# A decoder layer on one core: the experts' tiles change from 256 to 128 rows, each expert's first tile leaves the loop, and second choices are gathered by batch

## The chip, the core and the metric

The program runs on one core of a Trainium2 chip. The core has five engines that run side by side: TensorE (PE for its matmuls, PEld for its loads of stationary operands), VectorE (DVE), ScalarE (ACT), GpSimd (POOL) and SyncE (SP), and 16 DMA engines that move data. The metric is the device time of one execution in microseconds (us). Lower is better.

## What is computed

The reference is one decoder layer on x of shape (8, 224, 512) in float32: a Mamba block, cross-attention on a context of 750 rows, and a mixture of four experts. Each of the three adds its result to x. The change touches the last one:

```python
def _L0_ffn_ref(x, rW1, rb1, rW2, rb2, We1, be1, We2, be2):   # x: (8, 224, 512), We1: (4, 512, 2048), We2: (4, 2048, 512)
    rh = jax.nn.gelu(x @ rW1 + rb1, approximate=False)
    router_probs = jax.nn.softmax(rh @ rW2 + rb2, axis=-1)
    expert_weights, expert_indices = jax.lax.top_k(router_probs, 2)
    one_hot = jax.nn.one_hot(expert_indices, E, dtype=x.dtype)
    token_mask = one_hot.sum(axis=2)
    combine_w = (one_hot * expert_weights[..., None]).sum(axis=2)
    out = jnp.zeros_like(x)
    for e in range(E):
        xi = x * token_mask[..., e:e + 1]
        h = jax.nn.gelu(xi @ We1[e] + be1[e], approximate=False)
        yo = h @ We2[e] + be2[e]
        out = out + yo * combine_w[..., e:e + 1]
    return out
```

Every one of the 1792 rows takes two of the four experts, so 3584 rows go through an expert. Evaluated on its inputs, the reference sends 383, 1011, 1368 and 822 rows to experts 0 to 3.

## The kernel before

The program has four stages, one function each: `mamba_in`, `state_space`, `attention` and `experts`. The attention stage ends with the router. It gives each row two slots in `xs_d`, a table in device memory with 1792 slots for each expert, scatters the normed rows there (L1316), and counts each expert's tiles into `tiles_i` (`count_tiles`, L1464 on: `taken` compares the tile starts with the number of rows, `tiles[:, 0]` has the tiles of an expert and `tiles[:, 1]` the tiles before it).

`experts` (L1884) then does for each expert the tiles that its count asks for. Every engine runs the same frame, `expert_tiles` (L1969): read the two counts into registers (`counts`, L1965, its loads are L1967), do `first`, then a loop over all EG possible tiles of the expert (L1975) in which a branch (L1976) skips the tiles that aren't taken. EG is 7, since a tile has GT = 256 rows.

A tile is worked as follows.
- SP loads the tile's rows of `xs_d` into `xt` (L1994), one tile ahead. PE turns them by transposes with the identity (`tokens`, L2210, eight for a tile). The program keeps float32 accuracy by splitting every operand into a high part of type fp32r and the low rest. ACT writes the high part `xTh` (L2164) and DVE the low part `xTl` (L2116).
- The hidden layer has 2048 columns in HC = 16 chunks of 128. For chunk c, PE does the first layer: four blocks of the contraction with three products each (`products`, L2198 to L2200: high by high, high by low, low by high), so 12 matmuls. The stationary operand is a 128x128 block of the weights `w1h` or `w1l`, and the rows of the tile move, 256 of them. ACT applies the Gelu twice (L2173 for the high part `hh`, L2174 back into `ps`), and DVE takes the difference `hl` (L2124).
- PE does the second layer of chunk c two chunks later (AHEAD = 2): here `hh` and `hl` are stationary and the 512 columns of `w2h` or `w2l` move. A tile has two halves of 128 rows (HALVES = 2), so 6 matmuls.
- After the last chunk DVE adds the bias (L2131) into `y`, and ACT's queue stores it back into `xs_d` (L2177).

A product's three matmuls and what stands in which operand:

```python
(sh, sl), (mh, ml) = stationary, moving
nc.tensor.matmul(out, sh, mh, start=first, stop=False)
nc.tensor.matmul(out, sh, ml, start=False, stop=False)
return nc.tensor.matmul(out, sl, mh, start=False, stop=last)
```

Weights come in chunks of 1 MB into `stage` (eight for each expert). The first chunks of expert 0 are split into high and low by ACT (L2155) and DVE (L2099), all later ones by POOL (L2024 high, L2026 low), which waits for the last use of the buffer by the expert before. The first split of the tokens of an expert and the two counts stand between the last tile of one expert and the first of the next. DVE also works out the gates (L2103 to L2105) before its first `hl`.

At the end the two results of each row are added to the attention's output: POOL gathers the first choices by index while the last expert works (`gather`, L2052 into `early`; scaled in L2068, added in L2070), and when the last tile is stored it gathers the second choices of all 16 groups of 112 rows (L2052 into `back`, which is a view of `w1l`). DVE adds them (L2146), and SP (L2005) and ACT (L2189) store the output.

## Time and profile before

| what | value |
|---|---|
| three runs | 2640.47, 2632.47, 2620.92 us (median 2632.47 us) |
| the profiled execution | 2644.08 us |
| its span, first to last instruction | 2642.3 us |
| mean granted TensorE clock | 0.949 of 2.4 GHz |
| PE busy | 2374.5 us (90% of the span), 14400 matmuls |
| PEld busy | 2006.9 us (76%) |
| DVE, ACT, POOL busy | 1458.0 us (55%), 1237.7 us (47%), 1383.3 us (52%) |
| `experts` | from about 1793 us of the span to its end |

PE is busy through most of the span; how much of that is real work for the array the busy share doesn't say, since matmuls are pipelined and their shown lengths overlap. The pace of matmuls is therefore read from starts: how many start in how many us. A row's idle time is that of its engine just before the instruction, with what released it. The 1.7 us between the span and the execution's time are launch and end.

### The profile page before, as it was taken

The numbers are of one execution on the slowest core, as the hardware profiler recorded it, in microseconds if no ns is written. First come the engines' busy times: TensorE is split into PE (matmuls) and PEld (weight loads), VectorE is DVE, ScalarE is ACT, GpSimd is POOL, SyncE is SP. The second block draws the span as 40 slices with busy tenths as digits, with TensorE's granted clock in tenths as the row PEclk, the third lists the DMA queues.
The fourth block names the chain that finished last, engine by engine and source line by source line (L and its number), as shares of the span: only waits on it lengthen the run. The fifth ranks groups of instructions, "written<-read, shape, count | busy, mean of one in ns | idle before, by whom it ended". The sixth has DMA issues, their size and how long they took to land. (4 is left out here: it accounts for less than half of the span.)

```text
span 2642.3 us, 39584 instructions
## 1 busy us (share of the span) xinstructions
PE 2374.5 (90%) x14400; PEld 2006.9 (76%) x14400; DVE 1458.0 (55%) x2036; ACT 1237.7 (47%) x2659; POOL 1383.3 (52%) x952
## 2 busy tenths in 40 slices
PE   6999589999999998799999998975999989998994
PEld 5867389999999995566676666645888888888883
DVE  7804589999999993556776667634211211211212
ACT  4335477778877752344454445323233233333331
POOL 2413477877787871555656565635640640019812
PEclk9999789999999999799999999877999999999997
DMA  4326856656676564644555455415220220003303
GB/s 109 135 65 212 261 177 206 195 178 207 202 209 198 171 202 129 174 113 111 129 137 137 111 128 132 124 35 174 92 91 16 87 96 16 24 31 104 109 27 119
DMA packets 235987, 341.74 MB, mean 129 GB/s; under 512 B 34702, under 2 KB 164302, under 8 KB 234686
## 3 DMA queue, kind: packets, MB, share of 16 engines
q1 hardware_dynamic: 213246, 279.89, 37.2%
q0 software_dynamic: 13728, 47.19, 5.6%
q10 hardware_dynamic: 8864, 12.72, 1.4%
q8 instruction: 87, 1.43, 0.2%
q14 instruction: 62, 0.51, 0.1%
HBM read 212.08 MB, written 127.65 MB: 129 GB/s over the span
## 5 line engine op out<-in xcount | busy, mean ns | idle before, releaser
L956 DVE TENSOR_TENSOR_SCAN s_h<-s_decay,s_ub 128x928 f32<-128x928 f32 x256 | 527.5, 2080 | 17.5 <-PE s_ub L983 7.8
L994 PE MATMUL s_yps<-s_hc,identity 128*128 128x224 f32 x2016 | 425.8, 354 | 3.2 <-POOL s_hc L829 2.8
L2124 DVE TENSOR_TENSOR e_hl<-e_ps,e_hh 128x256 fp32r<-128x256 f32 x256 | 108.6, 425 | 571.5 <-ACT e_ps L2174 571.0
L882 ACT ACTIVATE s_decay<-s_dt,s_A 128x224 f32<-128x224 f32 x1024 | 387.9, 472 | 1.6 <-DMA s_dt<-dt_d 1.6
L994 PEld LDWEIGHTS s_yps<-s_hc,identity 128*128 128x128 f32 x2016 | 363.8, 191 | 5.4 <-POOL s_hc L829 4.7
L1338 DVE TENSOR_REDUCE t_nmax<-t_ps 112x1 fp32r<-112x752 f32 x256 | 240.2, 938 | 219.4 <-PE t_ps L1677 218.7
L1294 POOL TENSOR_TENSOR t_part<-t_pT 125x672 f32<-125x672 f32 x128 | 207.1, 1618 | 271.3 <-ACT t_pT L1582 268.9
L2173 ACT ACTIVATE e_hh<-e_ps,e_b 128x256 fp32r<-128x256 f32 x256 | 122.0, 477 | 433.0 <-PE e_ps L2200 432.8
L2198 PE MATMUL e_ps<-e_xTh,e_w1h 128*128 128x256 f32 x1024 | 293.1, 286 | 24.1 <-DVE e_xTl L2116 24.1
L1582 ACT ACTIVATE t_pT<-t_ps 125x448 f32<-125x448 f32 x384 | 181.1, 546 | 254.8 <-PE t_ps L1703 251.3
L2199 PE MATMUL e_ps<-e_xTl,e_w1h 128*128 128x256 f32 x1024 | 292.0, 285 | 0.0
L2200 PE MATMUL e_ps<-e_xTh,e_w1l 128*128 128x256 f32 x1024 | 291.0, 284 | 0.0
L829 POOL TENSOR_TENSOR s_hc<-s_h,carry 128x896 f32<-128x896 f32 x128 | 248.0, 1950 | 71.1 <-DVE s_h L956 49.7
L829 POOL TENSOR_TENSOR s_hc<-s_h,s_Cc 128x896 f32<-128x896 f32 x128 | 248.0, 1948 | 68.4 <-DVE s_h L956 49.7
L2024 POOL TENSOR_TENSOR e_w1h<-carry,e_one 128x2048 fp32r<-128x2048 f32 x13 | 46.9, 3611 | 376.5 <-PE e_ps L2200 376.3
L2198 PE MATMUL e_ps<-e_w2h,e_hh 128*128 128x512 f32 x512 | 206.0, 402 | 22.4 <-DVE e_hl L2124 22.4
L2198 PEld LDWEIGHTS e_ps<-e_xTh,e_w1h 128*128 128x128 f32 x1024 | 197.6, 193 | 35.0 <-issue 25.2
L1677 PE MATMUL t_ps<-t_k,t_q 96*112 96x376 f32 x512 | 186.9, 448 | 31.4 <-DVE t_nmax L1338 23.3
L2199 PEld LDWEIGHTS e_ps<-e_xTl,e_w1h 128*128 128x128 f32 x1024 | 197.4, 193 | 9.3
L2200 PE MATMUL e_ps<-e_w2h,e_hl 128*128 128x512 f32 x512 | 202.7, 396 | 0.0
L2199 PE MATMUL e_ps<-e_w2l,e_hh 128*128 128x512 f32 x512 | 202.2, 395 | 0.0
L2200 PEld LDWEIGHTS e_ps<-e_xTh,e_w1l 128*128 128x128 f32 x1024 | 198.9, 194 | 0.0
(242 smaller groups left out, 4611.2 us busy)
## 6 DMA issues: line engine op xcount, KB each, us to landing
s_ut<-ut_d SPq DMA_DIRECT2D x192, 128.0 KB, 3.3
carry<-in_L_ffn_We POOLq DMA_DIRECT2D x24, 1024.0 KB, 5.7
t_k<-kh_d SPq DMA_DIRECT2D x64, 375.0 KB, 6.5
xs_d<-s_zero SPq DMA_DIRECT2D x30, 512.0 KB
ut_d<-a_x SPq DMA_DIRECT2D x32, 448.0 KB, 5.5
kh_d<-s_kh SPq DMA_DIRECT2D x32, 375.0 KB, 3.0
kl_d<-s_kl SPq DMA_DIRECT2D x32, 375.0 KB, 3.6
v_d<-s_v SPq DMA_DIRECT2D x48, 250.0 KB
```

The costliest lines, as they stand in the source:

```text
L829: nc.gpsimd.tensor_tensor(hc[:, u % 2, k], h[:, k, :, 2:SLOT], Cc[b % 2][:, k], ALU.mult).then_inc(hc_done, 1)
L882: ins = nc.scalar.activation(decay[:, u % 2, :, n, 2:SLOT], dts[:, u % 2].rearrange("p (s t) -> p s t", s=NSEG), ACT.Exp, scale=A[:, u % C ...
L956: nc.vector.tensor_tensor_scan(h[:, k].rearrange("p n t -> p (n t)"), decay[:, u % 2, k].rearrange("p n t -> p (n t)"), ub[:, s % 2, AT:AT ...
L994: ins = nc.tensor.matmul(yps[:, u % 2, 0:L], ident[:], hc[:, u % 2, :, n], start=(n == 0), stop=(n == NS - 1))
L1294: nc.gpsimd.tensor_tensor(part[:], p[:, 0:3], p[:, 3:6], ALU.add).then_inc(sum_step, 1)
L1338: nc.vector.tensor_reduce(nmax[:, u, h:h + 1], ps[0:TT, 0:2, 0:EVEN], AX.XY, ALU.max, negate=True).then_inc(max_done, 1)
L1582: nc.scalar.activation(pT[:, g % PT, 2 * i:2 * i + 2], ps[0:CT, TURN_BANK + i, 0:2 * L].rearrange("p (i t) -> p i t", i=2), ACT.Exp).then_ ...
L1677: ins = nc.tensor.matmul(ps[0:TT, i, 0:EVEN], q3[0:ROWS3, b % 2, h, u * TT:(u + 1) * TT], k3[0:ROWS3, J % 2, h % 4, i * (CTX - EVEN):i * ( ...
L2173: nc.scalar.activation(hh[:, c % RING], hidden_in, ACT.Gelu, bias=bias).then_inc(S["h_high"], 1)
L2198: nc.tensor.matmul(out, sh, mh, start=first, stop=False)
L2199: nc.tensor.matmul(out, sh, ml, start=False, stop=False)
L2200: return nc.tensor.matmul(out, sl, mh, start=False, stop=last)
```

## The change

Tiles have 128 rows (GT = 128, EG = 14), so `xt`, `xTh`, `xTl`, `hh`, `hl` and `y` are half as long, a first-layer matmul moves 128 columns instead of 256, and a second-layer chunk has 3 matmuls instead of 6. The second layer runs three chunks behind (AHEAD = 3). The rows of a tile are turned at its step 8 instead of at its end.

Each expert's first tile is written out ahead of the loop (`first`), with rows of its own (`xf`, `fTh`, `fTl`, bank 7 of `ps`), which PE turns at step 12 of the first tile of the expert before and which ACT and DVE split at that tile's end. The loop has EG - 1 = 13 iterations, and `taken` counts only the tiles after the first.

The weights' chunks are split anew between the engines: POOL splits the first-layer chunks and an expert's first second-layer chunk; ACT and DVE split the other three second-layer chunks in halves, among the hidden chunks 1, 5 and 9 of an expert's first tile (for expert 0 chunks at 5, 9 and 13). `w2h` and `w2l` have a fifth part so that the next expert's first chunk has a place. SP loads these chunks, `b2` comes one expert at a time, and SP rather than ACT stores `y`.

Second choices are gathered by batch: DVE works out how many tiles of the last expert cover the rows of each of the batches 0 to 6 (`last_tiles`), and POOL waits for that many stores, gathers, scales and adds the two groups of that batch and stores its output, while the last expert still works. Only the last batch's two groups come after the last tile.

On PE the order within a tile changes. These are the rows in the loop's body around a second-layer chunk, in the kernel before (`e_w1h`, `e_w1l`, `e_w2h`, `e_w2l` are the weights, `e_ps` the banks that are written):

```order
L2200 MATMUL e_ps<-e_xTh,e_w1l 128x256
L1932 REGISTER_ALU
L2198 MATMUL e_ps<-e_w2h,e_hh 128x512
L2199 MATMUL e_ps<-e_w2l,e_hh 128x512
L2200 MATMUL e_ps<-e_w2h,e_hl 128x512
L2198 MATMUL e_ps<-e_w2h,e_hh 128x512
L2199 MATMUL e_ps<-e_w2l,e_hh 128x512
L2200 MATMUL e_ps<-e_w2h,e_hl 128x512
L2198 MATMUL e_ps<-e_xTh,e_w1h 128x256
```

And in the changed kernel, at the same place of its loop's body:

```order
L2298 MATMUL e_ps<-e_xTh,e_w1l 128x128
L1939 REGISTER_ALU
L2296 MATMUL e_ps<-e_w2h,e_hh 128x512
L2297 MATMUL e_ps<-e_w2l,e_hh 128x512
L2298 MATMUL e_ps<-e_w2h,e_hl 128x512
L2296 MATMUL e_ps<-e_xTh,e_w1h 128x128
```

The second layer has half as many rows for a tile of half the size. The first layer has 12 rows for each chunk in both (one ahead and one behind are shown here), each with half the moving columns.

The second place is POOL's end of the program. Before, it ends with the counts of the last expert and sixteen gathers (`e_w1l` is where `back` lies):

```order
L2068 TENSOR_SCALAR e_early<-e_early,e_gate 112x512
L2070 TENSOR_TENSOR carry<-carry,e_early 112x512
L1967 TENSOR_LOAD r_tiles_i
L1967 ISA x2
L1967 TENSOR_LOAD r_tiles_i
L1967 ISA x2
L1932 ISA
L2052 DMA e_w1l<-xs_d,r_index 112x512 x16
```

Now it ends with the last of seven batches and two gathers:

```order
L2104 DMA e_early<-xs_d,r_index 112x512 x2
L2113 TENSOR_SCALAR e_early<-e_early,e_gate 112x512
L2115 TENSOR_TENSOR carry<-carry,e_early 112x512
L2113 TENSOR_SCALAR e_early<-e_early,e_gate 112x512
L2115 TENSOR_TENSOR carry<-carry,e_early 112x512
L2134 DMA out<-carry 112x2x512
L1986 TENSOR_LOAD r_tiles_i
L1986 ISA x2
L1986 TENSOR_LOAD r_tiles_i
L1986 ISA x2
L1939 ISA
L2104 DMA e_early<-xs_d,r_index 112x512 x2
```

Fourteen of the sixteen gathers moved ahead of the wait for the last tile, with their scaling and adding, and these are POOL's now instead of DVE's.

The core of the diff:

```diff
-GT = 2 * P
+GT = P
...
-                nc.vector.tensor_reduce(tiles[:, 0, 0:E], taken[:], AX.X, ALU.add).then_inc(counted, 1)
+                nc.vector.tensor_reduce(tiles[:, 0, 0:E], taken[:, :, 1:EG], AX.X, ALU.add).then_inc(counted, 1)
...
-    AHEAD = 2
-    HALVES = GT // P
+    AHEAD = 3
+    EARLY = 3
...
-        w2h, w2l = (sb(n, [P, WG, CW, DM], F32R) for n in ("w2h", "w2l"))
+        w2h, w2l = (sb(n, [P, WG + 1, CW, DM], F32R) for n in ("w2h", "w2l"))
...
+        FROM_START = ((0, 0, 0), (0, 0, 1), (0, 1, 0), (0, 1, 1))
+        AMONG = [{5: (0, 2, 1), 9: (0, 3, 0), 13: (0, 3, 1)}] + [{1: (e, 1, 1), 5: (e, 2, 1), 9: (e, 3, 1)} for e in range(1, E)]
+        BY_ACT = list(FROM_START) + [AMONG[e][c] for e in range(E) for c in sorted(AMONG[e])]
+        BY_POOL = [(0, 2, 0), (1, 0, 1)] + [(e, g, 0) if g < WG else (e + 1, 0, 1) for e in range(1, E) for g in range(WG + (e + 1 < E))]
...
-            with eng.Fori(0, EG) as i:
+            with eng.Fori(0, EG - 1) as i:
                 with eng.If(i < taken_e):
-                    body(i, before + i, before + e + i)
+                    body(i, before + (e + 1) + i)
...
+                        load(e * EG + 1, n)
+                        wait_split(sp, (e, 0, 1))
+                        load_weights(sp, (e, 2, 1), S["w2_loaded0"])
+                        if e + 1 < E:
+                            load_first(e + 1)
+                            wait(sp, "y_done", n)
+                            load_b2(e + 1)
+                        wait_split(sp, (e, 1, 1))
+                        load_weights(sp, (e, 3, 1), S["w2_loaded1"])
+                    if e + 1 < E:
+                        for g in (2, 3):
+                            wait_split(sp, (e, g, 1))
+                            load_weights(sp, (e + 1, g - 2, 1), S[f"w2_loaded{g % 2}"])
+                    store(e * EG, n)
+                def tile(i, n):
+                    load(i + (e * EG + 2), n)
+                    store(i + (e * EG + 1), n)
+                expert_tiles(sp, e, first, tile)
...
+            split((0, 2, 0))
+            load_next((0, 2, 0))
+            load_next((0, 3, 0))
+            split((1, 0, 1))
             for e in range(1, E):
-                before = counts(pool, e)[1]
-                for n in range(2 * WG * e, 2 * WG * (e + 1)):
-                    g = n % (2 * WG) // 2
-                    wait(pool, "l2_mm" if n % 2 else "h_mm", before * HC + (g + 1) * CW - HC)
+                before = counts(pool, e)[1] + e
+                for g in range(WG):
+                    wait(pool, "h_mm", before * HC + (g + 1) * CW - HC)
                     pool.sem_inc(S["waited"])
-                    split(n)
-            pool.wait_ge(S["w_split"], 2 * WG * E)
+                    split((e, g, 0))
+                    load_next((e, g, 0))
+                if e + 1 < E:
+                    wait(pool, "l2_mm", before * HC)
+                    pool.sem_inc(S["waited"])
+                    split((e + 1, 0, 1))
...
+            for b in range(B - 1):
+                through = pool.value_load(through_i[0:1, b:b + 1], min_val=0, max_val=EG)
+                wait(pool, "y_stored", (before + through) * 16)
+                pool.sem_inc(S["waited"])
+                for i in (2 * b, 2 * b + 1):
+                    gather(1, i)
+                for i in (2 * b, 2 * b + 1):
+                    combine(1, i)
+                pool.wait_ge(S["early_combined"], NT + 2 * b + 2)
+                pool.dma_start(out[b].rearrange("(u p) d -> p u d", p=TT), stage[0:TT, b // 2, 2 * (b % 2):2 * (b % 2) + 2]).then_inc(out_early, 16)
+            total = counts(pool, E)[1] + E
+            wait(pool, "y_stored", total * 16)
             pool.sem_inc(S["waited"])
-            for i in range(NT):
-                gather(1, i, back[:, i // 4, i % 4], r_gathered[i // 4])
+            for i in (NT - 2, NT - 1):
+                gather(1, i)
+            pool.wait_ge(out_early, 16 * (B - 1))
...
+            def low_weights(chunk):
+                high, low = parts(chunk)
+                wait_weights(dve, chunk)
+                for half in range(2):
+                    two = slice(2 * half, 2 * half + 2)
+                    dve.wait_ge(S["w_high"], 2 * BY_ACT.index(chunk) + half + 1)
+                    v.tensor_tensor(low[:, two], raw(chunk)[:, two], high[:, two].bitcast(F32), ALU.subtract).then_inc(S["w_split"], 1)
...
+            def last_tiles():
+                then(v.tensor_scalar(seen[:], slot[0:1, 2:NT:2, E - 1], float(-(E - 1) * SLOTS), None, ALU.add))
+                then(v.tensor_tensor(cover, starts[:].unsqueeze(1).to_broadcast([1, B - 1, EG]),
+                                     seen[:].unsqueeze(2).to_broadcast([1, B - 1, EG]), ALU.is_lt))
+                then(v.tensor_reduce(seen[:], cover, AX.X, ALU.add))
+                v.tensor_copy(through_i[:], seen[:]).then_inc(S["known"], 1)
...
+                        low_hidden(n, c)
+                        if c in AMONG[e]:
+                            low_weights(AMONG[e][c])
+                        if c == 8:
+                            tokens(n)
+                        if e == 1 and c == 12:
+                            last_tiles()
+                    if e + 1 < E:
+                        first_tokens(e + 1)
+                    results(e, n)
+                def tile(i, n):
+                    for c in range(HC):
+                        low_hidden(n, c)
+                    tokens(n)
+                    results(e, n)
...
+            def first_tokens(e):
+                act.wait_ge(S["f_mm"], e + 1)
+                nc.scalar.activation(fTh[:].rearrange("p k t -> p (k t)"), ps[:, F_BANK], ACT.Copy).then_inc(S["f_high"], 1)
...
+                        hidden(e, n, c)
+                        if c in AMONG[e]:
+                            high_weights(AMONG[e][c])
+                        if c == 8:
+                            tokens(n)
+                    if e + 1 < E:
+                        first_tokens(e + 1)
+                def tile(i, n):
+                    for c in range(HC):
+                        hidden(e, n, c)
+                    tokens(n)
...
+            def layer1(e, n, c, xh, xl):
+                g, w = c // CW, slice(c % CW * P, c % CW * P + P)
+                wait(pe, "h_split", n * HC + c - RING + 1)
+                for q in range(KC):
+                    ins = products(ps[:, H_BANK + c % RING, 0:GT], (w1h[:, g, q, w], w1l[:, g, q, w]),
+                                   (xh[:, q], xl[:, q]), q == 0, q == KC - 1)
+                ins.then_inc(S["h_mm"], 1)
+            def layer2(e, n, c):
+                k = c % RING
+                high, low = parts((e, c // CW, 1))
+                if c == 0:
+                    wait(pe, "y_done", n)
+                wait(pe, "h_split", n * HC + c + 1)
+                ins = products(ps[:, Y_BANK], (hh[:, k], hl[:, k]), (high[:, c % CW], low[:, c % CW]), c == 0, c == HC - 1)
+                ins.then_inc(S["l2_mm"], 1)
...
+                def first(n):
+                    pe.wait_ge(S["f_split"], e + 1)
+                    for step in range(HC + AHEAD):
+                        c = step - AHEAD
+                        if step < HC:
+                            if step % CW == 0:
+                                wait_split(pe, (e, step // CW, 0))
+                            layer1(e, n, step, fTh, fTl)
+                        if step == 8:
+                            tokens(n)
+                        if step == 12 and e + 1 < E:
+                            first_tokens(e + 1)
+                        if c >= 0:
+                            if c % CW == 0:
+                                wait_split(pe, (e, c // CW, 1))
+                            layer2(e, n, c)
...
+                def tile(i, n):
+                    wait(pe, "x_split", n)
+                            layer1(e, n, step, xTh, xTl)
+                        if step == 8:
+                            tokens(n)
...
+                            layer2(e, n, step - AHEAD)
```

## Rows read from the trace of the kernel before

**Rows 1.** Chain of waits, pieces by time: start, us, what; two tile ends and the tail
```profile
2210.88 0.87 PE e_ps L2210 x8
...
2258.08 0.87 PE e_ps L2210 x8
...
2605.47 2.79 DMA xs_d<-e_y
...
2609.08 0.99 POOL e_w1l L2052
...
2628.93 7.30 DMA e_w1l<-xs_d,r_index
```

**Rows 2.** Groups of instructions from 1750 us on (busy, mean ns, idle before)
```profile
L2198 PE MATMUL e_ps<-e_xTh,e_w1h 128*128 128x256 f32 x1024 | 293.1, 286 | 24.1 <-DVE e_xTl L2116 24.1
...
L2198 PE MATMUL e_ps<-e_w2h,e_hh 128*128 128x512 f32 x512 | 206.0, 402 | 22.4 <-DVE e_hl L2124 22.4
...
L2173 ACT ACTIVATE e_hh<-e_ps,e_b 128x256 fp32r<-128x256 f32 x256 | 122.0, 477 | 433.0 <-PE e_ps L2200 432.8
...
L2116 DVE TENSOR_TENSOR e_xTl<-e_ps,e_xTh 128x512 fp32r<-128x512 f32 x40 | 25.8, 686 | 23.5 <-ACT e_xTh L2164 23.5
L2068 POOL TENSOR_SCALAR e_early<-e_early,e_gate 112x512 f32<-112x512 f32 x16 | 25.4, 1586 | 0.6
...
L2164 ACT ACTIVATE e_xTh<-e_ps 128x512 fp32r<-128x512 f32 x40 | 21.7, 596 | 4.5 <-PE e_ps L2210 3.5
```

**Rows 3.** Timeline of PE, one chunk's step: start, length, instruction
```profile
2000.96 0.28 PE L2198 MATMUL e_ps<-e_xTh,e_w1h 128*128 128x256 f32 x1
...
2002.38 0.40 PE L2198 MATMUL e_ps<-e_w2h,e_hh 128*128 128x512 f32 x1
...
2003.78 0.28 PE L2198 MATMUL e_ps<-e_xTh,e_w1h 128*128 128x256 f32 x1
```

**Rows 4.** Timeline of PE, runs of narrow matmuls in other stages
```profile
992.84 7.29 PE L1004 MATMUL s_yps<-s_hc,identity 128*128 128x112 f32 x64
...
1200.26 0.27 PE L1689 MATMUL t_ps<-t_turner,t_nmax 112*2 112x112 f32 x2
...
1202.29 0.81 PE L1703 MATMUL t_ps<-t_q,t_k 98*125 98x224 f32 x6
```

**Rows 5.** Lengths of one, ns min/median/max, by line
```profile
L1689 PE MATMUL t_ps<-t_turner,t_nmax x128: 212/217/378, 1047.1 to 1725.6; 112*2 112x112 f32 x128
L1703 PE MATMUL t_ps<-t_q,t_k x768: 263/272/695, 1049.3 to 1729.2; 98*125 98x224 f32 x192
```

**Rows 6.** Groups of weight loads, shapes apart (mean ns before the second bar)
```profile
L2198 PEld LDWEIGHTS e_ps<-e_xTh,e_w1h 128*128 128x128 f32 x1024 | 197.6, 193 | 35.0 <-issue 25.2
...
L1689 PEld LDWEIGHTS t_ps<-t_turner,t_nmax 112*2 112x2 f32 x128 | 11.1, 87 | 7.3 <-issue 2.0
```

**Rows 7.** Busy time by stretch: PE, PEld, DVE, ACT, POOL, granted clock, DMA
```profile
992.70:999.80 7.10, 7.10 (x65) 7.10 (x64) 0.85 (x2) 0.00 (x0) 1.56 (x1) 1.00 0.17 52
```

**Rows 8.** Timelines of ACT and PE around the change from one tile to the next
```profile
2265.73 1.28 ACT L2173 ACT_TABLE_LOAD   x1 [5.66 <-issue]
...
2268.35 0.50 PE L2198 MATMUL e_ps<-e_w2h,e_hh 128*128 128x512 f32 x1 [0.98 <-DVE e_hl L2124]
```

**Rows 9.** Timeline of PE at the change from expert 0 to 1 and 1 to 2
```profile
1913.54 1.09 PE L2210 MATMUL e_ps<-identity,e_xt 128*128 128x128 f32 x8 [1.80 <-issue]
1921.21 0.58 PE L2198 MATMUL e_ps<-e_xTh,e_w1h 128*128 128x256 f32 x1 [6.59 <-DVE e_xTl L2116]
...
2110.92 1.09 PE L2210 MATMUL e_ps<-identity,e_xt 128*128 128x128 f32 x8 [0.30 <-issue]
```

**Rows 10.** Timelines of DVE and POOL at the start of the experts
```profile
1808.25 4.59 DVE L2103 TENSOR_TENSOR e_eq<-r_slot,r_choice 112x64 f32<-112x64 f32 x1
...
1812.88 0.22 DVE L2104 TENSOR_TENSOR e_eq<-e_eq,r_pm 112x64 f32<-112x64 f32 x1
...
1807.50 5.26 POOL L2026 TENSOR_TENSOR e_w1l<-carry,e_w1h 128x2048 fp32r<-128x2048 f32 x1 [13.50 <-ACT e_w1h L2155]
```

More of the change, by code:

```diff
@@ L2080, in _ @@
             start(dve, "step x_split h_split y_done combined")
+            v = nc.vector
             step = [0]
@@ L2191, in _ @@
+            wait(act, "combined", 2)
+            act.dma_start(out_v[NT - 1], stage[0:TT, (NT - 1) // 4, (NT - 1) % 4]).then_inc(S["out_stored"], 16)
         @block.tensor
```

351 lines of the change are left out of this document (173 added, 178 removed).

## The prediction, made before the changed kernel ran

> **What bounds the kernel now.** I read the views in this order: the chain of waits, the groups of instructions, the timeline of PE, and then everything in the trace that tells the pace of a narrow matmul.
>
> The chain ends with 37 us of tail, and before it runs along PE through the experts [rows 1]. The tail: the last tile is stored (2605.47), sixteen gathers are issued one by one from 2609.08, the last lands 7.30 us after 2628.93, and the sums and the store end the span at 2642.3. In front of it, one tile follows the other in 47.2 us (2210.88 to 2258.08). The groups show why: each first-layer product has 1024 matmuls and each second-layer product 512, so 1024 / 64 = 16 tiles ran, and PE's idle time in front of them is 24.1 + 22.4 us in all [rows 2]. So PE bounds this stage: what the change does to the matmuls counts in full, and what it saves elsewhere is at most those 46 us, the cold clock behind them, and the tail.
>
> One step of the loop (a chunk's first layer, and the second layer of another) takes 2.82 us, from 2000.96 to 2003.78 [rows 3]. Its 12 matmuls of 256 columns take 1.42 us, 118 ns each; its 6 of 512 columns take 1.40 us, 233 ns each. Sixteen steps are 45.1 us, eight transposes 0.87 us [rows 1], and the remaining 1.2 us is the wait for the first `hl` of the tile: ACT loads a table for 1.28 us when it starts on the tile, and PE idles 0.98 us for DVE behind that [rows 8].
>
> **The change, part by part.**
>
> *Number of tiles.* The reference sends 383, 1011, 1368 and 822 rows to the experts. In tiles of 256 that is 2 + 4 + 6 + 4 = 16, as the trace has it. In tiles of 128 it is 3 + 8 + 11 + 7 = 29. The rows worked through fall from 4096 to 3712, by 9%.
>
> *Second layer.* Here the tile's rows are the stationary side, and 512 columns still move. So a chunk has 3 matmuls of 233 ns instead of 6: 0.70 us.
>
> *First layer.* The weights are stationary, and each of the 12 matmuls still needs its own load of 128 columns; only the moving side shrinks to 128. What does such a matmul take? The trace has no fp32r matmul with 128 stationary and 128 moving columns, so I bound it.
> - From below, if only its moving columns counted: L1689 moves 112 columns against 2 stationary ones, and the second of a pair starts 0.27 - 0.217 = 0.053 us after the first [rows 4, 5]. From 53 ns at 112 columns to 233 ns at 512 is 0.45 ns for a column, so 60 ns for 128.
> - From above, the 118 ns of today.
> - Nearest rows, with 128 or nearly 128 stationary columns: L1004, which moves 112 columns, runs 64 matmuls in 7.29 us, 0.275 us of which is the last one's own length: 7.02 / 63 = 111 ns. L1703 (fp32r, 125 stationary, 224 moving) starts six in 0.81 - 0.27 = 0.54 us: 108 ns [rows 4, 5]. The load itself lasts 87 ns with 2 columns and 193 ns with 128 [rows 6], so 106 ns more for 126 columns: a load occupies its path for about 108 ns, whatever moves.
>
> I take 111 ns. Halving the moving columns then saves 7 ns of 118, and the first layer, which was done once for 256 rows, is done twice. A chunk's first layer is 12 x 111 = 1.34 us, a step 2.04 us, sixteen steps 32.6 us, and four transposes 0.44 us: 33.0 us for a tile.
>
> The Trainium skill has a rule by which this would come out otherwise: "TensorE: Matmul & The Clock Gate", section "Back-to-back issue gap", gives about 81 ns for each matmul in a sustained stream of loads and matmuls of 128 columns. By it a tile would take 27.2 us. The rows at 108 and 111 ns don't agree with it, so I keep it as a rival.
>
> *From one tile to the next.* With AHEAD = 3 and the rows turned at step 8, what follows the last first-layer chunk is: two activations (under 1 us at 256 columns), the copy of 0.60 us and the subtraction of 0.69 us [rows 2], about 2.3 us in all, beside four second-layer chunks of 0.70 us on PE. ACT's table load lies beside the four first-layer chunks (5.3 us) that now precede the first second-layer one. So I expect most of the 1.2 us to go; bounds 0 and 1.3 us, taken 0.2 us. A tile then takes 33.2 us. Queued behind the subtraction on DVE are the bias and the loop's branch, which nobody waits for before the next tile's first `hl`.
>
> Sum of the tiles: 29 x 33.2 - 16 x 47.2 = 963 - 755 = **+208 us**.
>
> *From one expert to the next.* Each of the three changes costs the kernel before about 10 us over an ordinary tile: PE waits 6.6 us (at the first) for the first split of the tokens, after up to 1.8 us for its own branches, and comes out at half clock (a first matmul of 0.58 us instead of 0.28) [rows 9]. The token wait goes. What is late next is PE's own sequencer: with 5 skipped iterations it was 1.80 us late, with 3 only 0.30 us, so 0.75 us for each one skipped. Of 13 iterations it will skip 11, 6 and 3: 6.3 + 2.6 + 0.3 = 9 us. I add 6 us for the half clock behind the first two and 1.3 us for the extra transposes: 16 us instead of 31, **-15 us**, between -25 and 0.
>
> *Weights on DVE.* The low halves move into the first tile of an expert, beside POOL's splits. A DVE instruction with two inputs in SBUF doesn't run beside POOL: the one at 1808.25 took 4.59 us and ended with POOL's, which had begun at 1807.50 and lasted 5.26 us; the like-sized one behind it took 0.22 us [rows 10]. POOL's splits of the fourth chunk lie in the first 8 us of an expert's first tile, where DVE's first low half falls due; `hl` of the next chunk is queued behind it, and PE has about 4 us in hand. I take 1.5 us for each of three experts, **+4 us**, between 0 and 25 (three times a full split of 8.3 us).
>
> The Trainium skill says of this in "SBUF — State Buffer", section "Who interferes with whom", that GpSimd and such an operation of VectorE exclude each other for a whole instruction. The row of 4.59 us agrees with it. By that rule POOL can also be the one that waits, which would not reach PE here.
>
> *The start.* The gates' instructions no longer wait for two splits of POOL but for one: **-3 us**, between -6 and 0.
>
> *The tail.* Two gathers instead of sixteen remain: 14 x 1.24 us (the mean from 2609.08 to 2628.93 over 16) = 17 us, and a smaller burst lands sooner by some 3 us: **-21 us**, between -17 and -25. The fourteen others go to POOL beside the last expert. At about 1 us to issue and 1.6 us to scale [rows 2], no more to add, a group costs some 4 us, 30 groups 120 us, while the last expert's seven tiles take 232 us. So they hide.
>
> *Sum.* 208 - 15 + 4 - 3 - 21 = **+173 us**. On the profiled execution: 2644.1 + 173 = 2817 us. That execution lies 11.6 us above the median of the three runs, and I forecast against the median: 2632.5 + 173 = **2805 us**, 6.6% slower.
>
> **The rivals.**
>
> *A, the loads hide, and it is faster.* If the next load ran wholly beside the matmul before it, a first-layer matmul would take the 60 ns of its moving columns. There are 29 x 192 = 5568 of them, so 51 ns x 5568 = 284 us less: 2521 us. It decides from 80 ns down: 173 us / 5568 = 31 ns under 111. For it speaks that PEld always runs beside PE; against it both runs of narrow matmuls [rows 4], one in each format.
>
> *B, the loads hide in part.* If 31 of the 51 ns between the two bounds hid, a matmul would take 80 ns and the whole 5568 x 31 ns = 173 us less: 2632 us, no change. The same rows speak against it; for it, that no row has just this shape. The Trainium skill's 81 ns, named above, is nearly this case.
>
> *C, the handover stays.* If ACT's table load and branch still make PE wait 1.3 us a tile, and the matmuls stay at 118 ns as at 256 columns, it is 28 x 1.1 + 5568 x 0.007 = 31 + 39 = 70 us more: 2875 us. The first chunk of a tile is ready four chunks before its use now, which speaks against the wait; that today's 118 ns may come from memory rather than from columns speaks for the pace.
>
> *D, the clock.* The array now streams columns for a smaller part of the time (60 of 111 ns in the first layer). If the granted clock fell to 1.2 GHz in some tiles, each of them would take about 33 us more; five of them make 2970 us. Against it: in the stretch of L1004, which moves 112 columns in 111 ns, the granted clock was 1.00 [rows 7].
>
> **How the numbers follow.** Forecast 0.78, A 0.05, B 0.03, C 0.10, D 0.04. The range goes by the bounds: 108 ns instead of 111 takes 17 us off, and changes between experts without a late sequencer 9 more, with a tail and start at their best 7 more, so 2770; upwards the handover (31), half of the pace to 118 (20) and the collisions' and experts' upper ends in part give 2865. A measurement of this kernel can tell about 1%, 26 us, from no change. Faster by more than that is A (0.05), within it B (0.03), slower the rest (0.92).
>
> **What would show it.** In the changed kernel's profile: 5568 first-layer matmuls with 128x128 outputs that start 111 ns apart, their loads still about 193 ns long; a step of 2.04 us; tiles 33.2 us apart; 29 of them; idle of PE before L2296 with its largest single gaps where experts change, 6 us at the first; `w_split` waits of PE near nothing; two gathers behind the last store and about 16 us from it to the end. It would be wrong if the matmuls start less than 80 ns apart, or if the router's counts give other than 29 tiles (33 us for each).

## The result, and the profile after

The changed kernel takes 2839.45 us, the median of four runs from 2829.45 to 2844.61, beside 2632.89 us for the kernel before. The medians lie 207 us apart; the ratio on record is 1.0763, with an interval from 1.0732 to 1.0795, which is 201 us of the time before. 173 us had been forecast. The sign and the main mechanism (more matmuls at nearly the same pace each) were as forecast. The sum came out 28 us short by the ratio and 34 by the medians, and behind that stand larger errors of both signs.

The groups of instructions of the changed kernel, from 1780 us on (line, engine, operation, shapes, count, busy us and mean ns, idle before), answer to [rows 2] and [rows 6]:

```profile
L2298 PE MATMUL e_ps<-e_xTh,e_w1l 128*128 128x128 f32 x1600 | 440.2, 275 | 0.0
...
L2296 PEld LDWEIGHTS e_ps<-e_xTh,e_w1h 128*128 128x128 f32 x1600 | 305.8, 191 | 15.2
...
L2296 PE MATMUL e_ps<-e_w2h,e_hh 128*128 128x512 f32 x464 | 209.1, 451 | 4.1 <-DVE e_hl L2193 4.0
...
L2298 PE MATMUL e_ps<-e_fTh,e_w1l 128*128 128x128 f32 x256 | 88.1, 344 | 0.0
```

The first-layer matmuls are split over two tiles (`xTh` in the loop, `fTh` in an expert's first tile) and over three lines for the three products. 3 x (1600 + 256) = 5568 of them ran, so there were 29 tiles, as forecast; 464 / 16 = 29 says the same of the second layer. A load still takes 191 ns. The groups already hold a warning: a matmul of the same shape lasted 275 ns in the loop and 344 ns in the first tiles.

One step in the timeline of PE (start, length, instruction), the counterpart of [rows 3]:

```profile
2024.27 0.22 PE L2296 MATMUL e_ps<-e_xTh,e_w1h 128*128 128x128 f32 x1
2024.32 0.28 PE L2297 MATMUL e_ps<-e_xTl,e_w1h 128*128 128x128 f32 x1
2024.44 0.28 PE L2298 MATMUL e_ps<-e_xTh,e_w1l 128*128 128x128 f32 x1
...
2025.55 0.44 PE L2296 MATMUL e_ps<-e_w2h,e_hh 128*128 128x512 f32 x1
...
2026.30 0.22 PE L2296 MATMUL e_ps<-e_xTh,e_w1h 128*128 128x128 f32 x1
```

The step takes 2.03 us (2024.27 to 2026.30; 2.04 forecast). In it the narrow matmuls follow each other after 110 to 114 ns, in the median 112 (111 forecast). The one exception is the first, whose successor starts 50 ns later: the first one's own load had started at 2024.04, beside the last matmul of 512 columns.

The chain of waits by time (start, us, what) gives the tile and the tail, the counterparts of [rows 1]:

```profile
2672.48 0.46 PE e_ps L2311 x4
...
2705.46 0.46 PE e_ps L2311 x4
...
2822.07 0.70 DVE e_y L2199
2822.93 2.02 DMA xs_d<-e_y
2824.99 0.81 issue
2825.80 0.34 POOL e_early L2104
2826.26 0.83 POOLq L1901
2827.09 3.35 DMA e_early<-xs_d,r_index
2830.54 0.75 DVE carry L2235
```

L2311 turns the next tile's rows, once a tile: 32.98 us apart. Behind the last tile's sum at 2822.07 come one store, two gathers and one landing of 3.35 us, where there were sixteen gathers and one of 7.30 us. From that sum to the end it is 12.0 us; in the kernel before it was 37.7 us (2604.6 to 2642.3).

Who PE waited for from 1780 us on (line, releaser: us in total, times, longest):

```profile
PE e_ps L2304 <- DMA e_xf<-xs_d: 16.2, 1, 16.2
PE e_ps L2296 <- issue: 14.8, 3, 8.1
PE e_ps L2296 <- DVE e_hl L2193: 4.0, 1, 4.0
PE e_ps L2296 <- DVE e_fTl L2182: 1.5, 1, 1.5
```

The first is in the start. There is no wait of 1 us a tile for `hl` any more, against the 22.4 us of `hl` and 24.1 us of `xTl` in [rows 2]. The three changes between experts are left, and nothing but PE's own sequencer makes it late there.

The last view counts most. Busy time by stretch (PE, PEld, DVE, ACT, POOL, granted clock, DMA): the first 33 us of expert 1's first tile, the like stretch behind it, the first 32 us of expert 2's first tile, and an ordinary tile:

```profile
1925.40:1958.70 33.30, 33.30 (x139) 31.56 (x139) 7.95 (x14) 9.81 (x23) 7.14 (x4) 0.50 0.46 150
1958.70:1990.30 31.60, 31.60 (x236) 29.61 (x236) 8.76 (x23) 11.29 (x33) 2.48 (x1) 1.00 0.16 51
2210.05:2242.00 31.95, 31.95 (x132) 30.21 (x133) 7.95 (x14) 9.81 (x23) 9.62 (x4) 0.50 0.52 172
2023.30:2056.20 32.90, 32.90 (x245) 30.79 (x244) 6.05 (x18) 10.08 (x33) 0.00 (x0) 1.00 0.05 16
```

PE is busy throughout in all four. But in the first and third row the granted clock is 0.50 (1.2 GHz), and PE gets through 139 and 132 matmuls where it does 236 to 245 at 1.00 (2.4 GHz). The clock record has 0.50 from 1921.2 to 1958.7 and from 2207.9 to 2242.0, and at the start until 1842.7. The kernel before had its clock back 3 to 6 us after it set off again: its stretches at 0.50 end at 1825.4, 1924.4, 2125.7 and 2419.3.

*The account.* The two profiled executions differ by 191.7 us of span, but stages ahead of the experts, which the change leaves alone, ran 10 us shorter in the later one. The experts' stage itself is 201.7 us longer, and that lies between the 201 us of the ratio and the 207 of the medians. It splits so:

- Tiles at full clock: 29 x 32.97 - 16 x 47.2 = 956.1 - 755.2 = +200.9 us (forecast +208).
- From the stage's start to the first second-layer matmul: 26.6 before, 21.6 after, -5 us (forecast -3).
- The tail: 37.7 before, 12.0 after, -25.7 us (forecast -21).
- What is left of the stretch from the first second-layer matmul to the last sum: 784.7 - 755.2 = 29.5 us before, 1017.2 - 956.1 = 61.1 us after, +31.6 us. The forecast had -15 for the changes of expert and +4 for DVE and POOL, that is -11. Half of the +31.6 comes from the three changes of expert: over ordinary tiles they cost 31 us before and 47 after, where 16 had been forecast. The other half comes from expert 0's first tile.

The last line is the error. In the three low stretches, 37.8, 33.3 and 32 us of work went by at half clock, more than half of a first tile each time, at 3.84 us a step instead of 2.03. That costs 103 x (1 - 2.03 / 3.84) = 48 us; before, about 20 us of work at half clock cost 10. So 38 us more went to the clock.

### The profile page after: what moved, and what is told of

Read it like the earlier page. It is cut to its first block and busy times, and to the rows that moved or that the text cites. A ratio compares the mean times of both kernels' runs of the same rounds, so it can differ in the third digit from the quotient of the medians.

```text
span 2834.0 us, 46222 instructions
## 1 busy us (share of the span) xinstructions
PE 2625.0 (93%) x16724; PEld 2267.5 (80%) x16724; DVE 1492.3 (53%) x2252; ACT 1300.9 (46%) x3076; POOL 1324.4 (47%) x953
## 5 line engine op out<-in xcount | busy, mean ns | idle before, releaser
L2193 DVE TENSOR_TENSOR e_hl<-e_ps,e_hh 128x128 fp32r<-128x128 f32 x464 | 134.7, 291 | 758.9 <-ACT e_ps L2261 758.6
L2260 ACT ACTIVATE e_hh<-e_ps,e_b 128x128 fp32r<-128x128 f32 x464 | 170.5, 367 | 708.2 <-PE e_ps L2298 708.1
L2298 PE MATMUL e_ps<-e_xTh,e_w1l 128*128 128x128 f32 x1600 | 440.2, 275 | 0.0
L2297 PE MATMUL e_ps<-e_xTl,e_w1h 128*128 128x128 f32 x1600 | 439.9, 275 | 0.0
L2296 PE MATMUL e_ps<-e_xTh,e_w1h 128*128 128x128 f32 x1600 | 422.2, 264 | 0.0
L2296 PEld LDWEIGHTS e_ps<-e_xTh,e_w1h 128*128 128x128 f32 x1600 | 305.8, 191 | 15.2
L2297 PEld LDWEIGHTS e_ps<-e_xTl,e_w1h 128*128 128x128 f32 x1600 | 305.8, 191 | 13.7
L2298 PEld LDWEIGHTS e_ps<-e_xTh,e_w1l 128*128 128x128 f32 x1600 | 306.9, 192 | 0.0
L829 POOL TENSOR_TENSOR s_hc<-s_h,carry 128x896 f32<-128x896 f32 x128 | 247.9, 1947 | 68.4 <-DVE s_h L956 47.2
L2297 PE MATMUL e_ps<-e_w2l,e_hh 128*128 128x512 f32 x464 | 188.9, 407 | 0.0
L2298 PE MATMUL e_ps<-e_w2h,e_hl 128*128 128x512 f32 x464 | 187.5, 404 | 0.0
```

What stands on the lines that cost most here:

```text
L829: nc.gpsimd.tensor_tensor(hc[:, u % 2, k], h[:, k, :, 2:SLOT], Cc[b % 2][:, k], ALU.mult).then_inc(hc_done, 1)
L2260: nc.scalar.activation(hh[:, c % RING], hidden_in, ACT.Gelu, bias=bias).then_inc(S["h_high"], 1)
```

## The experiments

Two theories stood behind the first four runs. *Pace*: the 112 ns of a first-layer matmul are its load of 128 stationary columns, whatever moves, so the first layer of half a tile costs nearly as much as that of a whole one. *Clock*: some 38 us more than before come from first tiles that stay at half clock for long when it is narrow matmuls that follow the pause. Rivals were that the moving side or the memory sets the pace, and that the clock's return does not depend on the matmuls at all.

**e1: all first-layer matmuls move 256 columns.** The same 128 rows are moved twice, so the tile, the loads and the number of matmuls stay.

```diff
-                    ins = products(ps[:, H_BANK + c % RING, 0:GT], (w1h[:, g, q, w], w1l[:, g, q, w]),
-                                   (xh[:, q], xl[:, q]), q == 0, q == KC - 1)
+                    if True:
+                        out = ps[:, H_BANK + c % RING, 0:2 * GT].rearrange("p (a t) -> p a t", a=2)
+                        moving = tuple(t[:, q].unsqueeze(1).to_broadcast([P, 2, GT]) for t in (xh, xl))
...
+                    ins = products(out, (w1h[:, g, q, w], w1l[:, g, q, w]), moving, q == 0, q == KC - 1)
```

> The changed kernel with every first-layer matmul given its 128 columns twice (256 moving columns, the second half written to unused columns of the same bank); the output is the same. Theory 1 (the load of 128 stationary columns sets the pace, and the narrow moving side keeps the granted clock low after a gap): a first-layer matmul goes from 111 to 118 ns, a tile from 33.0 to 34.3 us (+39 us over 29 tiles), and the stretches at half clock after a change of expert shrink from 33 us to under 10 (-35 us): about 2843 us. Rival A (the moving columns set the pace): a tile goes to over 43 us, over 3100 us. Rival B (the low clock depends on the gap alone, not on the columns): the tiles as in theory 1 and the low stretches stay over 30 us: about 2878 us.

Measured: 2848.06 us, ratio 1.080 (1.0762 to 1.0837). Twice the columns cost 7 ns: 119 ns a matmul, 34.37 us a tile. Over 29 tiles that is 41 us, yet the kernel is only 9 us slower than the changed one, because the clock came back. The stretches of e1 around PE's restart (1921.31) at expert 1:

```profile
1918.20:1925.00 6.80, 3.69 (x17) 3.70 (x18) 0.02 (x1) 0.60 (x2) 3.61 (x2) 0.50 0.27 84
1925.00:1958.00 33.00, 30.85 (x223) 28.91 (x223) 18.98 (x26) 14.50 (x36) 9.04 (x2) 1.00 0.47 167
```

The clock is low for 6.8 us, half of it idle, instead of 37.5 us. Both theories hold.

**e2: only the first tiles move 256 columns.** The same edit with `if xh is fTh:` in place of `if True:`, the other tiles as in the changed kernel.

> The same doubling of moving columns, but only in the four first tiles; the output is the same. Theory 1: +5 us for 768 matmuls at 7 ns, and the low-clock stretches after a change of expert shrink from 33 us to under 10, at the start from 38 us of work to about 6: -15, -12 and -12 us: about 2805 us. Rival B: 2844 us, low stretches as before.

Measured: 2816.56 us, ratio 1.0677 (1.0642 to 1.0713), 23 us less than the changed kernel. The stretches around the first change of expert:

```profile
1919.50:1926.50 7.00, 2.36 (x11) 1.56 (x9) 1.68 (x3) 0.66 (x2) 6.60 (x4) 1.00 0.44 125
1926.50:1933.30 6.80, 3.30 (x15) 3.31 (x16) 0.00 (x0) 0.27 (x1) 5.01 (x2) 0.50 0.24 74
1933.30:1960.60 27.30, 26.19 (x193) 24.64 (x191) 16.37 (x17) 14.00 (x35) 9.06 (x2) 1.00 0.50 181
```

PE restarts at 1930.00 after the same pause of 8.14 us and has its clock back 3.3 us later. The clock theory had asked for 2805, the rival for 2844. It lies nearer to the theory, and a part of the gain was missing. PE was faster in these tiles, and so it now waited in them for the splitting of the weights: 2.69 us at the start for a low half, and 1.81 and 2.10 us at the first two changes for an `hl` that was queued behind one (e4 shows the rows of such a wait). Behind the first and the last of these waits the clock fell again, for 3.4 us, 27 us after it had come back. The third change, which had kept its clock in the changed kernel after a pause of 2.23 us, now had a low stretch of 3.4 us after the same pause.

**e3: half of the first-layer matmuls move 64 columns.** This leaves a part of the first layer's sum out: for two of the four blocks of features, 64 of the 128 rows.

```diff
-                    ins = products(ps[:, H_BANK + c % RING, 0:GT], (w1h[:, g, q, w], w1l[:, g, q, w]),
-                                   (xh[:, q], xl[:, q]), q == 0, q == KC - 1)
+                    n_cols = GT // 2 if q in (1, 2) else GT
+                    ins = products(ps[:, H_BANK + c % RING, 0:n_cols], (w1h[:, g, q, w], w1l[:, g, q, w]),
+                                   (xh[:, q, 0:n_cols], xl[:, q, 0:n_cols]), q == 0, q == KC - 1)
```

> The changed kernel with only 64 moving columns in six of the twelve first-layer matmuls of a chunk (blocks 1 and 2 of the contraction); the other 64 columns of those products are left out of the sum. Theory 1: at the full clock those six still start 111 ns apart, a tile stays at 33.0 us; the granted clock may be low in more places. Rival A (moving columns count): 28 ns less for each of the six, 2.7 us less for a tile.

Measured, in one run: 3082.53 us. Where the clock was full, nothing was gained; a piece of PE's timeline there:

```profile
2144.68 0.28 PE L2298 MATMUL e_ps<-e_xTh,e_w1l 128*128 128x64 f32 x1
2144.79 0.28 PE L2296 MATMUL e_ps<-e_xTh,e_w1h 128*128 128x64 f32 x1
2144.90 0.28 PE L2297 MATMUL e_ps<-e_xTl,e_w1h 128*128 128x64 f32 x1
```

Matmuls of 64 columns start 110 ns apart, and full-clock tiles took 33.0 to 33.1 us, as with 128. So 64, 128 and 256 moving columns give 112, 112 and 119 ns: the pace is the load's. The 243 us above the changed kernel go with the clock: between the start and the last few us it was at 0.50 for 584 us instead of 72, and with 0.47 us of work lost in each of the 512 us more, that makes 241. Two stretches of its loop, neither with a pause of PE:

```profile
2144.00:2154.00 10.00, 10.00 (x75) 9.28 (x73) 2.64 (x7) 3.17 (x11) 0.00 (x0) 1.00 0.08 32
2164.00:2174.00 10.00, 10.00 (x40) 9.13 (x40) 0.88 (x3) 1.80 (x6) 0.00 (x0) 0.50 0.00 0
```

PE is busy all the time in both, and the clock fell in the middle of dense tiles, for 24 to 65 us at a time; such tiles took 42 to 57 us. That is the forecast's rival D, with fewer columns than the change has.

**e4: 32 extra transposes before each first tile.** Unlike e2, this feeds PE ahead of the tile, not in it.

```diff
                 def first(n):
+                    for k in range(32):
+                        nc.tensor.transpose(ps[:, 5, 0:P], ident[:], ident[:])
                     pe.wait_ge(S["f_split"], e + 1)
```

> The changed kernel with 32 extra transposes of the identity into an unused bank ahead of each first tile. Theory 1: the granted clock comes back during or right after the extra transposes (they stream 256 cycles each without a pause), so the first tile of experts 1 and 2 runs at full clock: its time falls from 55 us (one turning of rows to the next) to about 46, the extra transposes' own 5 us included; 2820 to 2835 us in all. Rival B: the first tiles stay at half clock and the extra work adds its 3.5 to 7 us each: 2850 to 2860 us.

Measured, in one run: 2848.88 us, no gain. The stretches at expert 1, where PE set off again at 1938.04:

```profile
1934.10:1941.00 6.90, 2.96 (x14) 2.97 (x15) 0.00 (x0) 0.00 (x0) 5.59 (x3) 0.51 0.32 104
1941.00:1971.60 30.60, 28.64 (x226) 27.18 (x224) 16.86 (x17) 14.23 (x35) 8.99 (x2) 1.00 0.45 162
1971.70:1985.30 13.60, 12.69 (x42) 11.05 (x43) 3.48 (x12) 1.71 (x5) 0.00 (x0) 0.50 0.23 79
```

The transposes brought the clock back 3 us after PE had set off, as expected. 30.6 us later it fell again, for 13.6 us. PE was not busy throughout there, as rows of DVE, POOL and PE show:

```profile
1962.80 9.56 DVE L2162 TENSOR_TENSOR e_w2l<-carry,e_w2h 128x1024 fp32r<-128x1024 f32 x2 [0.75 <-ACT e_w2h L2246]
...
1965.87 5.40 POOL L2066 TENSOR_TENSOR e_w2l<-carry,e_w2h 128x2048 fp32r<-128x2048 f32 x1
...
1972.61 0.80 PE L2296 MATMUL e_ps<-e_w2h,e_hh 128*128 128x512 f32 x1 [2.97 <-DVE e_hl L2193]
```

DVE's low half took 9.56 us beside POOL's splits, the next `hl` was queued behind it, and PE idled for 2.97 us, from 1969.64 on; the clock fell at 1971.7, within that wait. The same happened at the second change: a wait of 2.56 us, then 10.2 us at 0.50. With the transposes' own time the sum is nothing. A start at full clock alone is no cure: the tile then runs into this wait, and with 128 moving columns the clock stayed low for longer behind it (10.2 and 13.6 us) than with 256 in e1 and e2 (3.4 us, where it fell).

**e5: the kernel before with only the gathers by batch.** Tiles stay at 256 rows; the tail's sixteen second-choice gathers become fourteen early ones on POOL and two late.

```diff
+            for b in range(B - 1):
+                through = pool.value_load(through_i[0:1, b:b + 1], min_val=0, max_val=EG)
+                wait(pool, "y_stored", (before + through) * 16)
...
+                for i in (2 * b, 2 * b + 1):
+                    gather(1, i)
+                for i in (2 * b, 2 * b + 1):
+                    combine(1, i)
...
-            for i in range(NT):
-                gather(1, i, back[:, i // 4, i % 4], r_gathered[i // 4])
+            for i in (NT - 2, NT - 1):
+                gather(1, i)
```

> The kernel before (tiles of 256 rows) with one part of the change alone: second choices gathered, scaled and added by batch beside the last expert, two gathers left behind the last store. Theory: this part alone is worth what the tail gained in the changed kernel, 37.7 - 11.9 = 26 us (-24 to -27), ratio 0.990. Rival: POOL doesn't keep up, since the last expert has only four tiles of 47 us and the batches end in bursts at three stores; then the gain is under 15 us.

Measured: 2616.19 us beside 2636.61, ratio 0.9913 (0.9887 to 0.9939), -23 us by the ratio. The last pieces of its chain:

```profile
2601.75 2.73 DMA xs_d<-e_y
2604.52 0.81 issue
...
2606.61 3.31 DMA e_early<-xs_d,r_index
2610.02 0.75 DVE carry L2171
```

The tail is 12.6 us instead of 37.7. This part of the change is a gain by itself, and it nearly all arrives.

**e6: the kernel before with only the next expert's rows turned in the last tile.** The matmuls of the first tile are not moved out of the loop.

```diff
-            first(before + e)
+            first(before)
             with eng.Fori(0, EG) as i:
-                with eng.If(i < taken_e):
-                    body(i, before + i, before + e + i)
+                with eng.If((i + 1 < taken_e) if eng is nc.sync and e + 1 < E else (i < taken_e)):
+                    body(i, before + i, before + i)
...
-                    tokens(t)
                     if e == 0:
+                        tokens(t)
```

> The kernel before with the next expert's first rows loaded, turned and split in the last tile of the expert ahead (SP takes the row number of the next expert there), tiles of 256 rows and the loops as they were. Theory: the token wait of 6.6 to 7.8 us goes at three changes; what is late next is PE's own branches (1.8, 0.3, 0 us) and ACT, which stores y and skips iterations before its first activation (3 us at the first change); with 256 moving columns the clock is back within 7 us: the three changes cost 10 us over an ordinary tile instead of 31, -18 to -22 us, ratio 0.992. Rival: the half clock behind the changes costs what it costs in the changed kernel, and the gain is under 5 us.

Measured: 2617.54 us, ratio 0.9925 (0.9896 to 0.9954), -20 us by the ratio. The periods at the three changes are 52.3, 51.4 and 50.9 us in place of 47.2, and each has 3.4 us of low clock. With 256 columns moving the clock was back 3.1 us after the restart at the first change (1915.31 to 1918.4). The single pauses at the changes are also shorter than in the changed kernel, 3.2 us at most.

**e7: the kernel before with `AHEAD = 3`.**

```diff
-    AHEAD = 2
+    AHEAD = 3
```

> The kernel before with AHEAD = 3 alone. Theory: the wait of 1.2 us at the start of each tile goes, a tile takes 46.0 us instead of 47.2, 15 tiles: -17 us, ratio 0.9935. Rival: the wait only moves (to the split of the tokens, which DVE and ACT do at the tile's end): no change within 5 us.

Measured: 2623.19 us, ratio 0.9937 (0.9913 to 0.996), -17 us by the ratio, as expected. What PE waited for, before and with the edit, first the kernel before:

```profile
PE e_ps L2198 <- DVE e_hl L2124: 22.4, 13, 10.1
```

And e7:

```profile
PE e_ps L2198 <- DVE e_hl L2124: 8.9, 1, 8.9
```

Twelve waits of 1.0 us are gone, and a tile takes 45.95 us instead of 47.2.

**e8: e5, e6 and e7 together, on tiles of 256 rows.** The three edits above in one kernel.

> The three parts together on tiles of 256 rows: everything of the change that was measured as a gain, without the tiles of 128. Theory: the gains add, -25 - 20 - 17 = -62 us, about 2572 us, ratio 0.9765. Rival: two of them hide the same wait (ACT's late start after a change of expert lies beside the third chunk ahead), and it is nearer -50 us.

Measured: 2583.52 us (2575.13 to 2593.48), ratio 0.9797 (0.9769 to 0.9825): -53 us, faster than both kernels. It is between the forecast sum of the parts (-62) and the rival (-50). In the profiled executions the stage is 60 us shorter, and the parts alone take 25, 18 and 19 us off it, 62 in all: they nearly add. What can be seen to be missing is at the end, where POOL is late. Its timeline (start, length, instruction):

```profile
2542.64 0.98 POOL L2055 DMA_INDIRECT e_early<-xs_d,r_index  x1 [1.04 <-issue]
...
2553.63 0.99 POOL L2055 DMA_INDIRECT e_early<-xs_d,r_index  x1 [0.73 <-issue]
...
2561.61 1.26 POOL L2066 TENSOR_TENSOR carry<-carry,e_early 112x512 f32<-112x512 f32 x1
...
2565.19 0.98 POOL L2055 DMA_INDIRECT e_early<-xs_d,r_index  x1 [1.26 <-issue]
```

A batch takes POOL 11 us. DVE's last sum starts at 2556.8, but the last two gathers start at 2565.19: the tail is 16.5 us rather than the 12.6 of e5.

**e9: the changed kernel with 10 iterations of the loop instead of 13.** PE skips three iterations fewer at every change of expert.

```diff
-            with eng.Fori(0, EG - 1) as i:
+            with eng.Fori(0, 10) as i:
```

> The changed kernel with 10 instead of 13 iterations in each expert's loop (enough for the 11 tiles of the largest expert in these inputs, so nothing is left out here). Theory: each skipped iteration is 0.75 us of PE's sequencer, so the gaps of PE at the three changes of expert fall from 8.1, 4.4 and 2.2 us to 5.9, 2.2 and about 0.5; the granted clock still falls at the first change and stays low for the first tile there (narrow matmuls), and doesn't fall at the second, which saves its 16 us: -6 us from the gaps, about -20 in all, ratio to before 1.069. Rival: both low stretches stay, -6 us, 1.074.

Measured: 2816.34 us, ratio 1.0691 (1.0656 to 1.0726). PE's waits for its sequencer:

```profile
PE e_ps L2296 <- issue: 8.1, 2, 5.9
```

The longest fell from 8.1 to 5.9 us: 2.2 us for three iterations, 0.75 us each, the forecast's figure. In all they fell by 6.7 us, but the kernel is 19 us (by the ratios) to 23 us (by the medians) faster than the changed one, and its stage 22 us shorter in the trace. The other 15 come from the clock: at the second change, where a wait of 4.42 us had been followed by 34.1 us at 0.50, the clock stayed at 1.00. The two periods there, from one turning of rows (L2311) to the next, took 35.5 + 33.4 us instead of 51.6 + 34.6.

**e10: e9 and e2 together.**

> The same with the first tiles' first-layer matmuls widened to 256 moving columns (as in the run that widened the first tiles alone). Theory: gaps of 5.9, 2.2 and 0.5 us and low stretches under 10 us: the changes cost 7 us less than with 13 iterations, ratio to before 1.065.

Measured: 2806.12 us, ratio 1.0654 (1.0627 to 1.0681), as expected. With its low stretches down to 6.8 and 3.4 us, this is the changed kernel with nearly all of its clock. It is still 6.5% slower than before: what is left is the number of matmuls at nearly the old pace.

## Why the prediction was right, and where it was not

*Number of tiles, second layer, first layer.* Right. 29 tiles, 5568 matmuls, 2.03 us a step (2.04 forecast). Within the step two small errors cancel: the twelve narrow matmuls take 1.28 us (1.34 forecast, without the short first gap), the three wide ones 0.75 us (0.70). The 112 ns lie just above the two nearest rows, 108 and 111 [rows 4]. The rule of the Trainium skill in "TensorE: Matmul & The Clock Gate", section "Back-to-back issue gap" (81 ns), does not hold for these matmuls. With it rivals A and B fall: the pace was no faster with 128 or even 64 moving columns (the changed kernel, e3), so at these widths the moving side does not set it. The term of +208 measured +201; 7 us were too many because the handover, taken at 0.2 us a tile, is nothing.

*From one tile to the next.* Right in the number. e7 shows that starting the second layer one chunk later is enough for the 1.2 us a tile: ACT loads its table as often as before (19 times in the stage), and PE no longer waits. In the changed kernel the forecast's reason does not apply as it stands: ACT's table load was to lie beside other work, but its trace has a single one in the experts' stage, at 1793.4. How much of the gain there is the missing load and how much the later start was not separated. Rival C falls; its 118 ns turn up only where 256 columns move.

*From one expert to the next.* Wrong, mainly in one step: "I add 6 us for the half clock behind the first two". The sequencer's gaps were 8.13, 4.42 and 2.23 us against 6.3, 2.6 and 0.3, 5.6 us more in all. With e9's 5.9 they are 0.75 us for each of 11, 6, 3 and 8 skipped iterations, and nothing off. The price was right; the 1.95 us of cover that had been read out of the kernel before (1.80 us for 5 skipped, 0.30 for 3) was not there. The larger part is the clock: the half clock was carried over from the kernel before, where it ended 3 to 6 us after the restart. With 128 moving columns it lasted 32 to 38 us, at the start and at two of three changes. At the two changes it cost 31 us instead of 6, and at the start 18 (3 in the kernel before), for which the forecast had no term. Expected at the three changes was a gain of 15 us; they lost 16. e2 shows the cause by its cure: with the pause unchanged and only the first tiles' moving columns doubled, the low stretch shrank from 37.5 to 6.8 us. e9 shows the other condition: with a pause of 2.22 us instead of 4.42 at the second change the clock did not fall at all.

This was rival D in small. It had been priced at 33 us a tile (measured: 15 to 18, since the clock comes back within the tile), and refused because L1004 ran 112 columns at full clock [rows 7]. That row says that a running engine can keep its clock. It does not say that an engine regains it, which was the question at a restart.

*Weights on DVE.* The collision is there. The timeline of DVE at the start of the experts, the counterpart of [rows 10]:

```profile
1792.89 5.76 DVE L2162 TENSOR_TENSOR e_w2l<-carry,e_w2h 128x1024 fp32r<-128x1024 f32 x2
1798.58 4.54 DVE L2166 TENSOR_TENSOR e_eq<-r_slot,r_choice 112x64 f32<-112x64 f32 x1
```

Both lie beside POOL's splits, and the second is as slow as it was. But at the changes of expert no wait of PE stands behind a low half, so the +4 us were nothing. That was luck, and it hung on the half clock. At the first change of the changed kernel the low half that falls due beside POOL came only 35.6 us after PE's restart, at the end of POOL's splits (1961.18). In e2, with PE at full clock, it came 22.3 us after the restart. The row of the changed kernel:

```profile
1961.02 2.38 DVE L2162 TENSOR_TENSOR e_w2l<-carry,e_w2h 128x1024 fp32r<-128x1024 f32 x2 [0.75 <-ACT e_w2h L2246]
```

In e1, e2 and e4, with the first tile mostly at full clock, it took 8.8 to 9.6 us at both of the first two changes, and PE waited 1.8 to 3.0 us for `hl`, about the 1.5 us and more that had been taken. The one wait for `hl`, 4.0 us, is in the start.

*The start.* -5 us, at the better end of the range given.

*The tail.* -26 us instead of -21, just outside the term's own bounds. Both parts were underrated: the landing shrank by 4 us, from 7.30 to 3.35, and the gathers and sums that left the end were nearly 22 us, not 17. e5 gives about the same alone, and e8 shows where the cover ends: when the stage gets shorter, POOL's 11 us a batch come into view.

*Sum.* Tiles -7, changes, clock and collisions +43, start -2, tail -5: 29 us more than forecast, and the ratio says 28. The total lies inside the range, by errors that partly cancel.

The account also tells what the change is worth part by part. The +201 us of the tiles already contain what e7 gains; beside e7's tile of 45.95 us the smaller tile costs 29 x 32.97 - 16 x 45.95 = 221 us at full clock, and 38 us of clock with it. The other ideas gain 23, 20 and 17 us when made alone on 256-row tiles (e5, e6, e7), and the kernel with all three is the fastest here, 256 us faster than the changed one. Two parts of the change are not in e8 and were not made alone: the first tile written out ahead of the loop, and the new division of the weights' splits.

What stays open: why the clock fell after a pause of 2.2 us in e1, e2 and e10 and did not in the changed kernel and e9, and why it fell behind most of the waits of 1.7 to 3.0 us in the first tiles but not behind two of them (1.81 us in e2, 2.15 us in e1, both at the first change). The runs show when the clock fell, not what decides it.

## What to carry to other kernels

Halving the moving side of a product whose every matmul loads 128 fresh stationary columns saves almost nothing for each matmul, so count matmuls, not rows: 9% fewer rows cost 27% more time in the tiles. Read how long the clock stays low after a restart from a restart with the new shapes, not from a dense stretch and not from the old shapes. Where a change bundles a layout with several waits that it removes, make each alone on the old layout: here each of the three that were made alone was a gain, and the layout cost about ten times what any of them gave. And expect a faster stretch to meet waits that the slow one had covered.

## What the runs showed of the hardware that had not been expected

- Matmuls with 128 stationary columns of this format started 112, 112 and 119 ns apart with 64, 128 and 256 moving columns. At half clock all three were 213 ns apart (64 in e3, 128 in the changed kernel, 256 in e1).
- The clock fell with no pause of PE at all: in e3, with 64 columns in half of the first-layer matmuls, it was at 0.50 for 584 us of the experts' stage behind its start, in 14 stretches, 11 of which began while PE was busy.
- After a pause of 8 us the clock came back 3.3 us after the restart with 256 moving columns, and only 33 us after it with 128. After a pause of 5.9 us (e9, 128 columns) it fell, for 34.1 us. After a pause of 2.2 us it did not fall with 128 columns (changed kernel, e9), but fell for 3.4 us with 256 in the tile behind it (e1, e2, e10).
- Transposes alone brought the clock back 3 us after PE had set off (e4). It fell again 30.6 us later, within a wait of PE of 2.97 us.
- Two halves of a low part on DVE took 9.56 us beside POOL's splits (e4) and 2.38 us behind them (changed kernel).
- ACT loaded its table 19 times in the experts' stage of the kernel before and once in the changed one.
- A skipped iteration of a loop costs PE's sequencer 0.75 us, and in the changed kernel none of it was hidden.
